# Earlier loads of finished heads, one square root behind the sums, and a gate that comes ahead of the experts' first step

## What is computed

```python
h = _layernorm(x) * (1 + ca) + sa                  # ca ... gb: six modulation vectors
x = x + ga * _L1_attn_ref(h, ...)                  # 16 heads of 8, 256-token causal mask after the softmax,
                                                   # residual, then a layer norm with gamma, beta ("n3")
h = _layernorm(x) * (1 + cb) + sb                  # "n4"
x = x + gb * _L1_ffn_ref(h, ...)

def _more_forward(x, Wg, bg, W1, b1, W2, b2):      # in _L1_ffn_ref
    cur = x
    for r in range(4):
        logits = flat @ Wg[r] + bg[r]
        vals, idx = top_k(logits, 2); w = softmax(vals)
        cw = sum(one_hot(idx, 4) * w)              # the gate: a weight per token and expert
        hmid = gelu(einsum('nh,ehf->enf', flat, W1) + b1)
        y = einsum('enf,efh->enh', hmid, W2) + b2
        cur = cur + einsum('ne,enh->nh', cw, y)
```

## Time and profile before

| | |
|---|---|
| median of 3 runs | 1754.97 us (1751.17 to 1760.66) |
| the profiled execution | 1752.73 us |
| its span, first to last instruction | 1750.9 us |
| TensorE, matmuls busy | 1561.3 us, 89% |
| VectorE busy | 1355.4 us, 77% |
| ScalarE busy | 1187.8 us, 68% |
| GpSimd busy | 624.0 us, 36% |
| mean granted TensorE clock | 0.935 |

### The profile page before, as it was taken

How to read it: one execution, slowest core, us unless ns; L and a number is a source line. 1 busy time by engine, 2 the same in 40 slices (tenths; PEclk the granted TensorE clock), 3 DMA queues, 4 the chain that set the end, 5 groups by cost and what they waited for, 6 DMA issues and landing times. The chain is left out here.

```text
span 1750.9 us, 29416 instructions
## 1 busy us (share of the span) xinstructions
PE 1561.3 (89%) x11136; PEld 851.8 (49%) x11136; DVE 1355.4 (77%) x1892; ACT 1187.8 (68%) x2302; POOL 624.0 (36%) x510
## 2 busy tenths in 40 slices
PE   6799999996689887799897999999988899999998
PEld 4122222222456664466652233333335677877776
DVE  4899999991677545776457899999956688999986
ACT  4368888885377743677534678787855667777775
POOL 2810000000477651676412143322212345555554
PEclk9689999999689988899997899999989899999999
DMA  2420010000111100111004221111010111111111
GB/s 76 108 91 20 20 35 20 1 1 32 40 31 32 32 25 19 25 28 34 12 8 108 91 69 23 23 29 23 11 13 10 49 41 45 49 43 48 44 46 52
DMA packets 68284, 66.05 MB, mean 38 GB/s; under 512 B 40840, under 2 KB 44296, under 8 KB 67632
## 3 DMA queue, kind: packets, MB, share of 16 engines
q1 hardware_dynamic: 67504, 61.94, 13.2%
q10 hardware_dynamic: 576, 2.16, 0.3%
q0 software_dynamic: 64, 0.07, 0.0%
HBM read 40.85 MB, written 14.81 MB: 32 GB/s over the span
## 5 line engine op out<-in xcount | busy, mean ns | idle before, releaser
L940 ACT ACTIVATE att_probs<-psum 128x512 f32<-128x512 f32 x1024 | 532.3, 604 | 167.0 <-PE psum L842 164.6
L955 DVE TENSOR_REDUCE att_neg_max<-psum 128x1 f32<-128x1024 f32 x512 | 600.9, 1219 | 34.3 <-PE psum L810 30.2
L810 PE MATMUL psum<-att_k_op,att_q_op 48*128 48x512 bf16 x1024 | 343.9, 406 | 17.1 <-DVE att_neg_max L955 10.0
L842 PE MATMUL psum<-att_q_op,att_k_op 50*128 50x512 bf16 x1024 | 316.4, 390 | 25.5 <-ACT att_probs L940 25.4
L2118 ACT ACTIVATE moe_hidden<-psum,moe_b 128x512 f32<-128x512 f32 x256 | 167.0, 690 | 94.1 <-PE psum L66 84.4
L842 PEld LDWEIGHTS psum<-att_q_op,att_k_op 50*128 50x128 bf16 x1024 | 77.6, 94 | 274.0 <-ACT att_probs L940 216.7
L860 PE MATMUL psum<-att_probs,att_v 128*32 128x512 f32 (+2 forms) x1664 | 203.0, 557 | 2.9 <-ACT att_sums L926 2.8
L59 DVE TENSOR_TENSOR moe_hidden_low<-moe_hidden,moe_hidden_high 128x512 fp32r<-128x512 f32 x192 | 191.9, 1046 | 8.1 <-ACT moe_hidden_high L2126 7.8
L1044 POOL TENSOR_TENSOR att_diag<-att_probs,att_triangle 128x512 f32<-128x512 f32 x64 | 81.0, 1266 | 282.1 <-ACT att_probs L940 145.5
L2177 POOL TENSOR_TENSOR moe_hidden_low<-moe_hidden,moe_hidden_high 128x512 fp32r<-128x512 f32 x64 | 97.3, 1521 | 173.0 <-ACT moe_hidden_high L2126 173.0
L810 PEld LDWEIGHTS psum<-att_k_op,att_q_op 48*128 48x128 bf16 x1024 | 74.0, 95 | 129.6 <-DVE att_neg_max L955 108.1
(11 more groups left out here) (255 smaller groups left out, 2856.1 us busy)
## 6 DMA issues: line engine op xcount, KB each, us to landing
moe_spread_weights<-gate_rows SPq DMA_DIRECT2D x64, 256.0 KB, 3.1
wl_v_shift<-wl_v SPq DMA_DIRECT2D x62, 128.0 KB, 2.2
att_q_op<-qk_parts SPq DMA_DIRECT2D x32, 192.0 KB, 3.2
att_k_op<-qk_parts SPq DMA_DIRECT2D x32, 192.0 KB, 4.2
qk_parts<-att_hi SPq DMA_DIRECT2D x12, 256.0 KB, 4.1
qk_parts<-att_hi SPq DMA_DIRECT2D x12, 192.0 KB, 2.9
att_q_op<-att_neg_rows SPq DMA_DIRECT2D x128, 2.0 KB
qk_parts<-att_mid SPq DMA_DIRECT2D x8, 256.0 KB, 3.2
```

The source lines that it names most:

```text
L810: mm = pe.matmul(buf[:, half * CHUNK:(half + 1) * CHUNK], q_op[it % RING][at_rows(p, MAX_ROW), j, t * P:(t + 1) * P], k_op[it % RING][at_r ...
L842: pe.matmul(st_bank[e % 3], k_op[it % RING][at_rows(p, MAX_ROW + 2), j, t * P:(t + 1) * P], q_op[it % RING][at_rows(p, MAX_ROW + 2), j, ha ...
L940: act.activation(probs[:, g % PB, h, :], st_bank[e % 3], ACT.Exp, scale=scale).then_inc(exp_done, 1)
L955: dve.tensor_reduce(neg[:, t, 2 * p + j:2 * p + j + 1], ring[e % 2], AX.X, ALU.max, negate=True).then_inc(ring_free, 1)
```

## The change

It has four parts.

1. `load_z(c)` for c = 0, 1, 2 is issued in units 2, 4, 6, directly behind the store of the second unit of its chunk, and no longer in units 3, 5, 7.
2. The square root of chunk 2 (n4) on ScalarE goes behind `take_sums` of the last half; those of chunks 0 and 1 stay.
3. TensorE computes `gate_logits(0)` ahead of the spread of chunk 2; `turn_weights(0)` moves from step 2 to step 0. ScalarE takes the gate's exponential ahead of all Gelus and copies the gate's rows out in step 1, no longer in step 3. VectorE ranks and normalises at once, ahead of the first hidden tile.
4. Chunk 3 of n3: `average3` goes from ahead of `down(1)` to behind it, the variance from ahead of `down(2)` to behind it, and VectorE's deviations from ahead of the loop into its first pass.

```diff
-                if behind and it in (3, 5, 7):
+                if behind and it in (2, 4, 6):
                     then.load_z(sp, it // 2 - 1)
...
             take_sums(HALVES - 1)
             if behind:
+                then.last_root(act)
                 then.on_act(act)
...
-        for c in range(3):
-            n4.spread_inverse(pe, c)
+        n4.spread_inverse(pe, 0)
+        n4.spread_inverse(pe, 1)
         gate_logits(0)
+        n4.spread_inverse(pe, 2)
         up(0)
         for n in range(STEPS):
             if n + 1 < STEPS:
                 up(n + 1)
-            if n == 1:
-                average3(pe, 3)
-            if n == 2:
+            if n == 0:
                 turn_weights(0)
-                n3.variance(pe, 3)
             if n == 3:
                 n3.spread_inverse(pe, 3)
...
             down(n)
             if n == 0:
                 turn_z(pe, 3)
+            if n == 1:
+                average3(pe, 3)
+            if n == 2:
+                n3.variance(pe, 3)
...
         if own.quarters - g == 1:
-            for c in range(3):
-                n4.root(act, c)
+            n4.root(act, 0)
+            n4.root(act, 1)
+
+    def last_root(act):
+        n4.root(act, 2)
...
         act.wait_ge(small_loaded, 16 * 4)
+        gate_exp(0)
         activate(0)
-        activate(1)
-        gate_exp(0)
-        for n in range(2, STEPS):
-            activate(n, 0 if n == 3 else None)
+        for n in range(1, STEPS):
+            activate(n, 0 if n == 1 else None)
...
         first_cast(0)
+        shift_logits(0)
+        for d in range(1, EXPERTS):
+            rank_logits(0, d)
+        keep_two(0)
         current(2)
-        shift_logits(0)
+        normalise(0)
         first_cast(1)
-        rank_logits(0, 1)
         cast_first(0)
         lower_hidden(0)
         compare(dve, 3)
         guard(dve, 3)
         first_cast(2)
-        rank_logits(0, 2)
         cast_first(1)
         lower_hidden(1)
         add_head(dve, 3)
-        rank_logits(0, 3)
-        keep_two(0)
-        normalise(0)
-        deviations(n3, dve, 3)
...
             if i == 1:
+                deviations(n3, dve, 3)
                 weigh(0)
```

More of the change, by code:

```diff
@@ L2401, in heads_and_experts @@
     then.tail_on_pe, then.last_variance, then.on_pe = tail_on_pe, last_variance, on_pe
-    then.tail_on_act, then.on_act = tail_on_act, on_act
+    then.tail_on_act, then.last_root, then.on_act = tail_on_act, last_root, on_act
     then.tail_on_dve, then.on_dve = tail_on_dve, on_dve
```

## The result

The change takes 1739.42 us (median of 6 runs, 1736.12 to 1742.83) against 1753.65 (6 runs): a ratio of 0.9912, 95% interval 0.9888 to 0.9935, so 14.2 us less. Six more runs of the same kernel gave 1739.08 and 0.9927 (0.9910 to 0.9945). The forecast was 1744.7, 10.3 us less: right in its range and its sign, and short by 3.9 us. (The time itself is 5.3 us under the forecast, because the kernel before has a median of 1753.65 over six runs, 1.3 us under the 1754.97 of the three runs that the forecast started from.)

What follows compares the result with a forecast made beforehand. TensorE bounds the experts' steady part; at the junction its waits for VectorE and lowered clock cost time. Terms -1.2 + 0.1 - 10.4 + 1.2 = -10.3 us gave a median of 1744.7 us, range 1737 to 1752.

Steps and rivals of the forecast that it cites:

- The steps: From up(0) to n4's chunk 3 variance: 12.4 us lost become 2.0, so -10.4 us (-4.6 to -11.5).
- The reserve at the reciprocal: Behind up(4): root and reciprocal of chunk 3 ready by 1372, TensorE asking near 1373, 1 us to spare.
- low parts beside GpSimd: Step 0 on VectorE: low parts, no longer a ranking operation, are blocked by GpSimd, about 1 us of the 2.0 lost.
- The loads: Attention's tail: heads loaded a unit sooner remove VectorE's 4.10 us and TensorE's 1.23 us waits, SyncE unharmed; -1.2 us.
- Root and gate up to up(0): End of attention to up(0): transposes 0.84 us sooner, used up by the gate; up(0) at +0.1, less the loads' 1.2.
- the clock's term: Around the gate: TensorE does little for 3.6 us, so one clock fall slows up(0); +1.2 us (0 to +2.9).
- (a): First steps: the wait moves to down(0) and chunk 3's spread, 5 us lost again, 1749.7 us; chance 0.20.
- (b): Attention's tail: the slow clock from 1304 to 1321 goes too, about 6 us more gained, 1738.7 us; chance 0.12.
- (c): Gate through step 3: TensorE stays at 1.2 GHz, 20 us lost, 1763.5 us; chance 0.04.
- (d): First steps: gate rows early but weigh(0) finds another wait, both stalls return in full, 1753.9 us; chance 0.04.

Runs made afterwards that it cites:

- late rows: The change with the gate's weights turned and its rows copied out two steps later, as before: 1747.59 us, 0.9957 of the kernel before.
- second profile: Profile of the change run once more without any edit: 1739.08 us, 0.9927 of the kernel before, span 1736.7 us.
- spread first: The change with the third spread of n4 put ahead of the gate's logits on TensorE: 1738.21 us, 0.9912 of the kernel before.
- Fillers at the gate: The change with all three n4 spreads ahead of the logits, plus six unused matmuls between spreads and logits: 1738.71 us, 0.9916 of the kernel before.
- loads and root alone: The kernel before with only the earlier loads and the root of chunk 2 behind the sums: 1750.13 us, 0.9979 of the kernel before.
- chunk 3 back: The change with chunk 3's mean, variance and VectorE's deviations put where they were: 1743.60 us, 0.9943 of the kernel before.
- gate alone: The kernel before with only the change's third part, the gate ahead of the first step: 1746.19 us, 0.9950 of the kernel before.
- turn behind down(8): Gate 1's weights turned behind down(8): 1731.62 us (0.9887) with n4's third spread ahead of the logits, 1737.95 us (0.9907) on the change as it is.

## Why the prediction was right, and where it was short

**The steps: right.** The term was -10.4 from a balance of TensorE's work. The two profiles gave -10.9 and -11.1: 36.65 and 36.53 us against 35.2 of work and 2.0 of losses. That the early rows carry it is shown by late rows: alone put back, they bring 8.4 us again, with waits of 6.25 and 4.73 us. Of the rest chunk 3's places are worth 1.2. The reserve at the reciprocal was real: in the first profile it was ready at 1373.62 and TensorE asked for it at 1375.49, 1.9 us later (forecast: 1). Mis-sized within the term were the low parts beside GpSimd: the three of step 0 took 3.99 us in the second profile against 1.90 for three beside nobody in the kernel before, so VectorE lost 2.1 us, where the prediction had about 1; TensorE felt little of it.

**The loads: right.** -1.2; both waits went, SyncE's queue moved nothing, and put back they cost 2.5 us, of the size of the runs' spread.

**Root and gate up to up(0): right where the clock is alike.** The sum said 1.1 us sooner without the clock's term. In the second profile up(0) starts 58.43 us after the mark against 59.51: 1.08 sooner, fall of 3.5 us included. In the first it starts 1.82 later. Reading the wait of 1.51 us at the logits, the spread should fit into it for nothing. It does, and is worth nothing: spread first moved up(0) and up(1) forward, and TensorE then waited for VectorE's low parts.

**The clock's term: of the wrong kind.** I took +1.2 for one fall at the gate. Fillers at the gate took that fall away and won nothing, because the first Gelu (behind the exponential and its two table loads) and VectorE's list both start from the logits and not from up(0): that price is 0. What does cost is a fall that slows transposes, spreads and logits ahead of them: 2.9 us to up(0) between the two profiles of one kernel. That belongs to the spread between executions (1736 to 1743), not to the sum.

**What was missed: the place behind the head.** I let the stretch behind n4's variance stand at its old length. It got 1.5 to 1.7 us shorter. Before, TensorE waited 2.43 us for gate 1's weights and then ran 3.5 us at half speed:

```profile
1416.50:1420.00 3.50, 1.07 (x6) 0.45 (x5) 3.16 (x13) 3.49 (x8) 0.67 (x1) 1.00 0.00 0
1420.00:1423.50 3.50, 3.50 (x10) 2.69 (x10) 3.50 (x4) 0.75 (x3) 2.80 (x2) 0.52 0.02 5
```

In the second profile of the change the same wait, 2.12 us, was followed by no fall (the stretches 1405 to 1408.5 and 1408.5 to 1412 shown with it: TensorE busy 1.45 of 3.5 us, then a clock of 1.00). All profiles that show the fall there have 356.6 to 356.9 us to the end; those with the same wait and no fall have 355.2 to 355.4. The split follows the edits: all five kernels that lack the early rows or chunk 3's places (before, late rows, loads and root alone, chunk 3 back, gate alone) have the fall, all seven profiles of the six kernels with both don't. With one profile of most that speaks for the change having brought it, not for how: chunk 3 back and gate alone fall after a wait of 2.13 and 2.14 us, the change doesn't after 2.12. With the turn behind down(8) neither wait nor fall is there.

**The sum.** Second profile against before: -0.4 ahead of the mark, -1.1 to up(0), -11.1 in the steps, -1.7 behind: -14.2 (1750.9 - 1736.7). The medians differ by as much; that one profile meets them to the tenth is chance. Against the forecast's -10.3 the steps gave 0.7 more, the clock's term 1.2, the stretch behind 1.7, and 0.4 is from ahead of the junction. For reference, the mark of before:

```profile
1286.91 0.40 PE L823 MATMUL psum<-ident,att_neg_max 128*32 128x128 f32 x8
```

**The rivals.** (a) did not come: no wait took the old ones' place within the steps. (b), the tail at full clock, did not come in either profile of the change, so that its 1738.7 lies nearer to the measured time than the forecast's 1744.7 is chance. But it can be seen in others: with a fall of 3.5 us in place of 17 (two of these three have another of 7 that begins just ahead of the transposes) the transposes come 2.6 to 3.4 us sooner (47.8 to 48.6 after the mark against 51.2). I had priced it at 6, since I counted TensorE's half speed and not ScalarE's exponentials behind their table load: TensorE waits 3.35 us for them there at full clock (loads and root alone), 1.83 at half (second profile of the change). (c) fell: in the change the longest fall from the gate on was 7 us. (d) fell with late rows.

**Low parts beside GpSimd, and the clock.** A low part that started at 1352.90 took 1.67 us and ended at 1354.57 while GpSimd's ran from 1352.61 to 1354.02; the same operation, beside nobody, took 0.69 before. It reads as the Trainium skill has it, "SBUF — State Buffer", section "SBUF: two separate sides": blocked until GpSimd was done, and over 0.55 us later, within 0.14 us of its own 0.69. The Trainium skill, "TensorE: Matmul & The Clock Gate", section "A second HAM failure mode: psum-queue depth-cycling", tells of a clock that falls and rises with frequent short idles. In the first profile it did fall twice around the gate, but TensorE was busy for all of the 3.5 us of the first fall and stood still once between the two, for 1.51 us, so no run shows that idles did it; in the change's steps 1 to 4, where I had put the price of that as rival (c), the clock was 1.00 throughout.

## What to carry to other kernels

Where an engine waits long for a transfer, look at what stands behind that wait in its list: here `weigh(0)` held the inverse root that TensorE needed, and starting the chain (rank, turn, copy, store, load) two steps sooner was worth 8.5 us without removing a single instruction of it. A balance of the bound engine's work against the stretch's length sized this gain better (10.4 of 11.1 us) than adding up the waits would have (7.8), since it takes in what the clock lost. And a fall of the clock costs only what TensorE's lateness reaches: fillers that kept the clock up, and an order that moved matmuls forward, gave nothing where VectorE's list and ScalarE's first Gelu came last. Before you order matmuls anew, look for the engine that works without a break from the last result that it got from TensorE: its list sets the pace.

## What the runs showed of the hardware

TensorE's clock fell in attention's tail in all fourteen profiles, for 17 to 25 us in ten of them, for 10.5 in one and for 3.5 in three, two of these without fillers; a wait of 2.1 to 2.4 us at gate 1 was followed by a fall in some kernels and not in others, with the kernel's own order the same there. Runs of one kernel spread over 2 to 12 us (up to 0.7%), and the longer ones tend to have the lower mean clock: of the change's six, the run of 1736.1 us has 0.941 and that of 1742.8 has 0.936. So edits of 1 to 2 us were told from the profile's distances and not from the medians. Not all of the spread lies in the stretch that the change touches: up to 5.7 us of it arose between 423 and 1015 us.
